# Graph network on one core: the bucket stage gathers a 16-row piece for 128 lists and an 8-row piece for the rest, with six buffers

## The reference

```python
def _denoise_gcn_layer(x, row, col, noise, nbW, nbb, selfW, selfb, attW, attb):
    f1 = x[row]
    f2 = x[col]
    h1 = jax.nn.relu(f1 @ nbW + nbb)
    h2 = jax.nn.relu(f2 @ selfW + selfb)
    log_alpha = jnp.concatenate([h1, h2], axis=1) @ attW + attb
    u = jnp.clip(noise, EPS_NOISE, 1.0 - EPS_NOISE)
    gate = jax.nn.sigmoid(jnp.log(u) - jnp.log1p(-u) + log_alpha)
    mask = jnp.clip(gate * (ZETA - GAMMA) + GAMMA, 0.0, 1.0)[:, 0]
    rowsum = jax.ops.segment_sum(mask, row, num_segments=N_NODES) + EPS_DEG
    d_inv_sqrt = jnp.clip(rowsum ** (-0.5), 0.0, 10.0)
    vals = mask * d_inv_sqrt[row] * d_inv_sqrt[col]
    msg = vals[:, None] * f2
    return jax.ops.segment_sum(msg, row, num_segments=N_NODES)
```

## Time and profile before

| what | value |
|---|---|
| median of 3 runs | 6465.84 us |
| the profiled execution's own time | 6478.92 us |
| its span | 6477.2 us |
| mean granted TensorE clock, share of full speed | 0.68 |
| busy share of PE, DVE, ACT, POOL | 69%, 83%, 39%, 18% |
| moved by DMA | 1154.51 MB, 178 GB/s over the span |
| bucket stage, first layer, from first gather issue to last output | 3304 to 4048 us |
| bucket stage, second layer | 5731 to 6472 us |

### The profile page before, as it was taken

The page is one execution under the profiler, slowest core; times in us unless marked ns, Lnnn a source line. Parts: engine busy times, 40 slices in busy tenths (PEclk is TensorE's granted clock), DMA queues, the critical chain, the costliest instruction groups (busy, mean ns, idle before and its releaser), DMA issues. The chain is left out here.

```text
span 6477.2 us, 167839 instructions
## 1 busy us (share of the span) xinstructions
PE 4475.7 (69%) x58388; PEld 3985.0 (62%) x58388; DVE 5351.0 (83%) x10813; ACT 2500.7 (39%) x5126; POOL 1167.5 (18%) x1562
## 2 busy tenths in 40 slices
PE   3777777775878887355557777978885355557776
PEld 2666666664568886344446666578885344446666
DVE  8999999996469998999976666079998999976666
ACT  2556666662345554355510000445553355510000
POOL 0000000000013332000024443023332000034443
PEclk6777777775555555677778888555555677778888
DMA  2000000000356665799978888066665799979988
GB/s 67 0 0 0 0 0 0 0 0 13 8 201 233 233 233 172 268 330 330 330 235 242 238 238 224 0 206 231 231 231 164 279 330 330 330 237 246 247 248 225
DMA packets 438063, 1154.51 MB, mean 178 GB/s; under 512 B 211241, under 2 KB 216974, under 8 KB 437402
## 3 DMA queue, kind: packets, MB, share of 16 engines
q1 hardware_dynamic: 316671, 549.97, 26.9%
q0 software_dynamic: 75264, 350.72, 20.0%
q10 hardware_dynamic: 46036, 252.74, 10.3%
HBM read 932.05 MB, written 279.36 MB: 187 GB/s over the span
## 5 line engine op out<-in xcount | busy, mean ns | idle before, releaser
L1587 PE MATMUL psG<-y_window,area 128*128 128x64 bf16 x14976 | 666.1, 217 | 783.5 <-DVE area L1235 669.1
L1587 PEld LDWEIGHTS psG<-y_window,area 128*128 128x128 bf16 x14976 | 622.4, 114 | 827.4 <-issue 507.3
L1600 PE MATMUL psG<-work,edge 112*128 112x192 bf16 x7104 | 811.1, 278 | 360.4 <-DVE edge L1270 358.6
L1600 PEld LDWEIGHTS psG<-work,edge 112*128 112x128 bf16 x7104 | 732.1, 151 | 438.9 <-DVE edge L1270 367.7
L582 POOL DMA_INDIRECT work<-msg_d,widx x444 | 488.1, 1099 | 2125.2 <-issue 1580.3
L638 ACT ACTIVATE work<-iota,work 128x149 bf16<-128x149 f32 x2496 | 789.0, 406 | 0.0
L1409 PE MATMUL psG<-area,work 128*128 128x112 bf16 x2496 | 551.3, 390 | 339.7 <-DVE area L967 339.7
L1409 PEld LDWEIGHTS psG<-area,work 128*128 128x128 bf16 x2496 | 357.6, 149 | 488.2 <-issue 343.8
L1402 PE MATMUL psG<-work,merge 128*128 128x148 bf16 x4992 | 542.5, 293 | 70.0 <-ACT work L638 70.0
L1402 PEld LDWEIGHTS psG<-work,merge 128*128 128x128 bf16 x4992 | 525.8, 131 | 92.7 <-issue 66.8
L1270 DVE TENSOR_TENSOR edge<-y_edge,ids 112x2048 bf16<-112x2048 int16 x444 | 544.2, 1226 | 15.4
(11 more groups left out here) (254 smaller groups left out, 8172.2 us busy)
## 6 DMA issues: line engine op xcount, KB each, us to landing
msg_d<-work ACTq DMA_DIRECT2D x312, 776.0 KB, 4.5
area<-rlo_d SPq DMA_DIRECT2D x312, 512.0 KB, 4.2
merge<-crel_d SPq DMA_DIRECT2D x312, 512.0 KB, 5.0
area<-crelp_d SPq DMA_DIRECT2D x312, 512.0 KB, 5.7
y_window<-y_d SPq DMA_DIRECT2D x312, 48.0 KB, 3.5
work<-msg_d,widx POOLq DMA_INDIRECT x444, 15.4
y_d<-cur SPq DMA_DIRECT2D x7, 1008.0 KB, 3.8
y_d<-work SPq DMA_DIRECT2D x7, 1008.0 KB, 4.8
```

The lines of the kernel that those rows point to most:

```text
L1587: ins = pe.matmul(psG[:, 2 * h + k // CH, k % CH * D:(k % CH + 1) * D], col_one_hots[:, h, k * P:(k + 1) * P], y_window[:, h, m * D:(m + 1 ...
L1600: ins = pe.matmul(psG[:, slot_, 0:MW], q_one_hots[slot_][0:WP, g, :, s], windows[slot_][0:WP, g, s, 0:MW], start=g == 0 and s == 0, stop=g ...
```

## The change

The window of a row piece is 8 rows (WIN), and a buffer holds 24 rows (WG = 3 groups of 8) on 128 partitions. The first gather takes 16 rows for lists 0 to 127. The second takes 8 rows (3104 bytes) per partition: on partitions 0 to 63 (THIRD) rows 17 to 24 of runs longer than 16, on 64 to 71 (up to FOURTH) rows 25 to 32 of runs longer than 24, on 72 to 99 rows 1 to 8 of the lists 128 to 155, and on 100 to 127 rows 9 to 16 of the same lists where the run is longer than 8. DVE makes all 24 one-hots of a bucket in one instruction, after both gathers; PE adds 24 products for each bucket. There are six buffers in place of four. Both gathers of a bucket are issued after one wait. The ranking at the start is done for two lengths, with 64 and 8 slots, and the slots of the second are filled by matmuls of their own. `is_local` now compares with 64 and 8.

```diff
-WIN = 16
-WG = 2
-WP = 112
-SLOTS = 4
-SPILL = WG * WP - T
+WIN = 8
+WG = 3
+SLOTS = 6
 TAIL = T - P
+THIRD, FOURTH = 64, P - 2 * TAIL
...
-                    for g in range(WG):
-                        wait(pool, half_summed, (n - SLOTS) * WG + g + 1)
+                    wait(pool, bucket_summed, n - SLOTS + 1)
+
+                    for g, rows in enumerate((range(0, 2 * WIN), range(2 * WIN, 3 * WIN))):
                         pool.nop(nofuse=True)
                         pool.indirect_dma_start(
-                            out=windows[par][0:WP, g, :, :].rearrange("p s w -> p (s w)"), out_offset=None, in_=msg_d,
-                            in_offset=bass.IndirectOffsetOnAxis(ap=widx[0:WP, g, b:b + 1], axis=0),
-                            bounds_check=T * TR - WIN, oob_is_err=False).then_inc(windows_loaded[par][g], 16)
+                            out=windows[par][:, rows.start:rows.stop, :].rearrange("p s w -> p (s w)"), out_offset=None, in_=msg_d,
+                            in_offset=bass.IndirectOffsetOnAxis(ap=widx[:, g, b:b + 1], axis=0),
+                            bounds_check=T * TR - len(rows), oob_is_err=False).then_inc(windows_loaded[par], 16)
...
-                dve.tensor_scalar(spills[h], runs[h], float(WIN), None, ALU.is_gt).then_inc(spills_ready, 1)
+                for k in range(2):
+                    ins = dve.tensor_scalar(spills[h][:, k * HI:(k + 1) * HI], runs[h], float((k + 2) * WIN), None, ALU.is_gt)
+                ins.then_inc(spills_ready, 1)
...
+            for h, (first, lanes) in enumerate(tiles):
+                dve.tensor_tensor(fourth_hots[h][0:lanes, :, :], iota[0:lanes, 0:FOURTH - THIRD].unsqueeze(1).to_broadcast([lanes, HI, FOURTH - THIRD]),
+                                  spill_slot[h][:, HI:2 * HI].unsqueeze(2).to_broadcast([lanes, HI, FOURTH - THIRD]), ALU.is_equal)
...
                 def bucket_hots(b, s, use):
                     n = L * HI + b
-                    for g in range(WG):
-                        dve.wait_ge(windows_loaded[s][g], use * 16)
-                        wait(dve, half_summed, (n - SLOTS) * WG + g + 1)
-                        dve.tensor_tensor(ids[0:WP, s, g * WIN:(g + 1) * WIN], windows[s][0:WP, g, :, MW].bitcast(i16),
-                                          shift[0:WP, g, bass.ds(b, 1)].to_broadcast([WP, WIN]), ALU.subtract).then_inc(ids_ready, 1)
-                        dve.wait_ge(ids_ready, n * WG + g + 1)
-                        dve.tensor_tensor(q_one_hots[s][0:WP, g, :, :], iota_rows[0:WP, :, :],
-                                          ids[0:WP, s, g * WIN:(g + 1) * WIN].unsqueeze(1).to_broadcast([WP, P, WIN]), ALU.is_equal).then_inc(q_hots_ready, 1)
+                    dve.wait_ge(windows_loaded[s], use * 32)
+                    wait(dve, bucket_summed, n - SLOTS + 1)
+                    dve.tensor_tensor(ids[:, s, :].rearrange("p (g s) -> p g s", g=WG), windows[s][:, :, MW].bitcast(i16).rearrange("p (g s) -> p g s", g=WG),
+                                      shift[:, :, bass.ds(b, 1)].to_broadcast([P, WG, WIN]), ALU.subtract).then_inc(ids_ready, 1)
+                    dve.wait_ge(ids_ready, n + 1)
+                    dve.tensor_tensor(q_one_hots[s], iota_rows.unsqueeze(1).to_broadcast([P, WG, P, WIN]),
+                                      ids[:, s, :].rearrange("p (g s) -> p g s", g=WG).unsqueeze(2).to_broadcast([P, WG, P, WIN]), ALU.is_equal).then_inc(q_hots_ready, 1)
...
-                    dve.memset(work[0:WP, :], 0.0).then_inc(windows_cleared, 1)
-                    dve.memset(area[0:WP, 0:WG * RW_], 0.0).then_inc(windows_cleared, 1)
+                    dve.memset(work[:, :], 0.0).then_inc(windows_cleared, 1)
+                    dve.memset(area[:, 0:2 * WG * RW_], 0.0).then_inc(windows_cleared, 1)
...
                     for h in range(2):
                         lanes = (P, TAIL)[h]
-                        ins = pe.matmul(psR[0:SPILL, 0, 3 * c:3 * c + 3], spill_hots[p_ % 2][h][0:lanes, b, :], row_parts[h][:, c, :], start=h == 0, stop=h == 1)
+                        pe.matmul(psR[0:THIRD, 0, 3 * c:3 * c + 3], spill_hots[p_ % 2][h][0:lanes, b, :], row_parts[h][:, c, :], start=h == 0, stop=h == 1)
+                    for h in range(2):
+                        lanes = (P, TAIL)[h]
+                        ins = pe.matmul(psR[THIRD:FOURTH, 0, 3 * c:3 * c + 3], fourth_hots[h][0:lanes, c, :], row_parts[h][:, c, :], start=h == 0, stop=h == 1)
...
-                        for g in range(WG):
-                            pe.wait_ge(q_hots_ready, n * WG + g + 1)
-                            for s in range(WIN):
-                                ins = pe.matmul(psG[:, slot_, 0:MW], q_one_hots[slot_][0:WP, g, :, s], windows[slot_][0:WP, g, s, 0:MW],
-                                                start=g == 0 and s == 0, stop=g == WG - 1 and s == WIN - 1)
-                            ins.then_inc(half_summed, 1)
+                        pe.wait_ge(q_hots_ready, n + 1)
+                        for r in range(WG * WIN):
+                            ins = pe.matmul(psG[:, slot_, 0:MW], q_one_hots[slot_][:, r // WIN, :, r % WIN], windows[slot_][:, r, 0:MW],
+                                            start=r == 0, stop=r == WG * WIN - 1)
+                        ins.then_inc(bucket_summed, 1)
```

More of the change, by code:

```diff
@@ L181, in build @@
         runs = [scratch[:, 296:296 + HI], scratch[0:TAIL, 443:443 + HI]]
[L182 to L187, removed]
+        spills = [scratch[:, 590:590 + HI].bitcast(bf16), scratch[0:TAIL, 738:738 + HI].bitcast(bf16)]
+        spill_slot = [scratch[:, 886:886 + HI].bitcast(bf16), scratch[0:TAIL, 1034:1034 + HI].bitcast(bf16)]
+        spill_row = [scratch[:, 1182:1182 + 2 * HI], scratch[0:TAIL, 1478:1478 + 2 * HI]]
+        row_parts = [area[0:lanes, at:at + 221].bitcast(bf16)[:, 0:3 * HI].rearrange("p (b m) -> p b m", m=3) for lanes, at in ((P, 0), (TAIL, 222))]
+        spilled, late_runs = scratch[:, 1774:1774 + HI], area[:, 444:444 + HI]
+        spill_hots = [[words(2 * NC + (2 * s + h) * PH * THIRD // 2, PH * THIRD // 2).bitcast(bf16).rearrange("p (b r) -> p b r", r=THIRD) for h in range(2)] for s in range(2)]
+        FW = HI * (FOURTH - THIRD) // 2
+        fourth_hots = [words(2 * NC + 2 * PH * THIRD + h * FW, FW).bitcast(bf16).rearrange("p (b r) -> p b r", b=HI) for h in range(2)]
         TB = (TBLOCKS + 1) * P
@@ L232, in build @@
         RW_ = WIN * MR // 2
-        windows = [t.bitcast(bf16).rearrange("p (g s w) -> p g s w", g=WG, s=WIN) for t in [work[:, h * WG * RW_:(h + 1) * WG * RW_] for h in range(3)] + [area[:, 0:WG * RW_]]]
-        q_one_hots = [t.rearrange("p (g n s) -> p g n s", g=WG, n=P) for t in [edge[:, 9 * NC + h * WG * P * WIN:9 * NC + (h + 1) * WG * P * WIN] for h in range(3)] + [merge_bf]]
-        iota_rows = y_edge[:, :, :, :].rearrange("p h k d -> p (h k d)").bitcast(i16).rearrange("p (n s) -> p n s", s=WIN)
+        HR_ = WG * P * WIN
+        windows = [t.bitcast(bf16).rearrange("p (r w) -> p r w", w=MR) for t in [work[:, h * WG * RW_:(h + 1) * WG * RW_] for h in range(4)] + [area[:, h * WG * RW_:(h + 1) * WG * RW_] for h in range(2)]]
+        q_one_hots = [t.rearrange("p (g n s) -> p g n s", g=WG, n=P) for t in [edge[:, 9 * NC + h * HR_:9 * NC + (h + 1) * HR_] for h in range(4)] + [merge_bf[:, 0:HR_], edge[:, 4 * NC:4 * NC + HR_]]]
+        iota_rows = y_edge[:, :, :, :].rearrange("p h k d -> p (h k d)").bitcast(i16)[:, 0:P * WIN].rearrange("p (n s) -> p n s", s=WIN)
         X = [work, cur]
@@ L274, in build @@
         y_fetched = [sem("y_fetched0"), sem("y_fetched1")]
-        table_loaded = [sem(f"table_loaded{k}") for k in range(4)]
         finish_step = sem("finish_step")
@@ L380, in _ @@
             sp.dma_start(tail_starts, start_d[P:T, :]).then_inc(starts_loaded, 16)
-            sp.dma_start(late_starts[SPILL:WP, :], start_d[WP:T, :]).then_inc(starts_loaded, 16)
+            for g in range(2):
+                sp.dma_start(late_starts[FOURTH + g * TAIL:FOURTH + (g + 1) * TAIL, :], start_d[P:T, :]).then_inc(starts_loaded, 16)
             whole = TBLOCKS * P * P
@@ L1004, in _ @@
                 link(dve.tensor_tensor(wide[0:lanes, 0:1], wide[0:lanes, 0:1], cnt[0:lanes, 0:1], ALU.max))
-                link(dve.tensor_tensor(spill_row[h], first[:, 0:HI], window_row[0:lanes, h:h + 1].to_broadcast([lanes, HI]), ALU.add))
-                link(dve.tensor_copy(row_parts[h][:, :, 0], spill_row[h]))
-                link(dve.tensor_tensor(spill_row[h], spill_row[h], row_parts[h][:, :, 0], ALU.subtract))
-                link(dve.tensor_copy(row_parts[h][:, :, 1], spill_row[h]))
@@ L1009, in _ @@
-                link(dve.tensor_tensor(row_parts[h][:, :, 2], spill_row[h], row_parts[h][:, :, 1], ALU.subtract))
+                row = spill_row[h][:, 0:HI]
+                link(dve.tensor_tensor(row, first[:, 0:HI], window_row[0:lanes, h:h + 1].to_broadcast([lanes, HI]), ALU.add))
+                link(dve.tensor_copy(row_parts[h][:, :, 0], row))
```

(9 more changed lines are left out.)

61 lines of the change are left out of this document (36 added, 25 removed).

## The result

The changed kernel takes 6106.57 us (median of 4 runs, 6092.52 to 6120.1); the kernel before took 6464.83 us beside it. The ratio is **0.9442** (95% interval 0.9415 to 0.9468), 358 us faster. The profiled execution took 6092.52 us; its span is 386.5 us shorter than that of before.

What follows compares the result with a forecast made beforehand. Gather DMA on the fullest engines was taken to bound the bucket stage. -171 + 42 + 5 + 1 + 5 = -118 us took the profiled 6478.9 to 6361, as median 6348 us; range 6200 to 6440.

Steps and rivals of the forecast that it cites:

- The change, part by part: the gathers: Bucket stage: scaling 0.356 us a piece, a bucket falls from 4.98 to 4.40 us, gaining 171 us.
- The fast and the slow end: Bucket stage: 4.27 us a bucket if the fullest DMA engine sets the pace, 4.49 us if all traffic together does.
- Rival 1: Gathers: on 128 partitions pieces get faster, at 23.7 GB/s 3.14 us a bucket, 5978 us in all; chance 0.13.
- DVE without waits for gathers: Bucket stage of the changed profile: a sign that pieces got faster or that DVE or PE became the bound.
- those are orderly copies, not gathers: Gathers: objection to expecting faster pieces from queue 10's 23.7 GB/s with stores of the same 6208 bytes.
- POOL: two issues of 0.98 us, at the worst 2.03: Bucket stage: POOL's gather issues take less than the 4.40 us of a bucket, so they cost nothing.
- Six buffers cost and bring nothing: Bucket stage: six buffers in place of four costed at nothing, as the fullest engines already never lacked work with four.
- rival 3: Bucket stage: DVE (comparison 3.5 us) or PE at low clock becomes the bound, 4.7 us a bucket, 6437 us; chance 0.11.
- PE's clock: Bucket stage: granted clock of 0.86 to 0.87 may be low more often; 24 products take 2.36 to 4.17 us.
- Rival 2: Second gather: half pieces cost as long as whole ones, 5.70 us a bucket, 6731 us in all; chance 0.12.
- The ranking: Start of the kernel: 294 more small PE products at 0.144 us cost 42 us, added DVE work ahead 5 us.
- the ends of the stage: Bucket stage, both layers: longer clearing of `area` and longer last comparison and products cost 5.4 us together.

## Why the prediction was right or wrong

**What bounds the kernel before: right in kind, wrong in one step.** The gathers' transfers did set the pace, and no other engine. The wrong step is "The change, part by part: the gathers": I took the 16.9 GB/s of a busy engine as a property of the gather and scaled with 0.356 us a piece. The fast and the slow end, 4.27 and 4.49 us, both kept it. It was a property of the gather to 112 partitions: one number set to 128 in the kernel before lifts it to 22.3 GB/s. That step is worth 4.40 - 3.57 = 0.83 us a bucket, 244 us, about the whole miss (241 us).

**Rival 1 was the case**, with 0.13. The row that spoke for it, queue 10 at 23.7 GB/s with the same 6208 bytes, was the right one; measured were 21.5. Its 3.14 us a bucket wasn't reached because its next bound was missing: from 3.57 us on it is POOL. For the same reason its sign "DVE without waits for gathers" didn't come: DVE still waited for one in 196 of 294 buckets, 211.5 us in all, now because it is issued late. The objection "those are orderly copies, not gathers" was no measurement; the same data gather at 22.3 GB/s.

**"POOL: two issues of 0.98 us, at the worst 2.03": wrong.** The mean is now 1.48 us. The earlier trace rows had the sign of it, a maximum of twice the median, and I took it for a worst case and not for a mechanism. Before, with issues spread over 4.98 us by waits for PE, a third of them started inside a comparison of 1.23 us (29 of 80 in the 200 us from 3500 us); now a comparison is 1.76 us long and more than half do (60 of 113).

**Six buffers cost and bring nothing: right**, though for another reason than the one given. **The bytes: right**, 316.89 MB against 316. **DVE's comparison: right**, 1.76 us against 1.84, and rival 3's slow comparison did not come; DVE is busy for 0.72 to 0.75. **PE's clock: wrong in sign.** I feared a lower granted clock; it rose from 0.86 and 0.87 to 0.93 and 0.95, although PE is busy for 0.68 in place of 0.73. Why isn't shown.

**Rival 2, half pieces paid by number: no.** The second gather's 8-row pieces didn't become a bound in any run; with a small comparison the whole bucket takes 2.87 us. Where such a piece stands as a packet of its own, in the change cut to 112 partitions, its median is 0.184 us, half of the 0.368 of a whole one there.

**The ranking: right in kind, 42 us forecast.** PE's block runs from 1552.48 us to 1622.06 us, when the next work begins:

```profile
1552.48 0.35 PE L1465 MATMUL psR<-area,work 128*64 128x3 bf16 x2 [14.65 <-DVE work L1041]
...
1622.06 4.32 PE L1452 MATMUL psG<-ident,work 128*128 128x128 f32 x19
```

That is 69.6 us where it was 42.42, so +27 us: a pair of products with eight columns of weights adds 0.19 us (2 x 0.095), cheaper than the 0.144 us I took for all. Ahead of it DVE took 4.7 us more (5 forecast); the tiny operations cost about nothing (1 forecast).

**The sum by its own terms:** -171 became -414; +42, +5, +1 became +27, +5, 0. The +5 for the ends of the stage became about -2: from the start of the clearing to the first output it took 27.8 and 28.1 us before and takes 26.7 both times with the change. The span fell by 386.5 us where 118 were forecast; some 2 us are left open. The range was too narrow because I let it reach only half-way to a rival whose mechanism, if it held, would hold whole.

## What to carry to other kernels

Let an indirect gather span all 128 partitions, even with empty lanes and more of them: here 16 partitions more were worth 388 us of 6465 with no fewer bytes to move. It was tried with pieces of 6208 and 3104 bytes on one core, and why it is so stays open. When a gather's busy engines are slower than those of a plain copy with pieces of the same size, that gap is a finding and not a constant to scale with. And when POOL issues beside long two-input comparisons on DVE, look at where the issues start: the gap between comparisons must hold a blocked issue's rest and the pause after it, and if it lacks a few tenths, a delay on purpose can pay, as it did here with 0.425 us and not with 0.225.

## What was unexpected about the hardware

A busy DMA engine moved 21.9 GB/s in gathers to 128 partitions and 15.8 to 16.5 GB/s in gathers to 64, 96 or 112, in one program in which only the gathered partitions differ. A gather issue that starts before a DVE comparison, or at most 0.04 us after its start, takes 1.00 us; one that starts 0.05 us after its start or later ends 0.87 us behind the comparison's end, whatever the wait. And 0.425 us of useless DVE work for each bucket, 125 us in all, made the kernel 148 us faster.
